# Two projections of an attention block as three rounded passes, and GpSimd's images and the gate's steps in another order

## The reference, cut to what matters

```python
xn = layernorm(x) * ln1_scale + ln1_bias              # over the 64 channels
q, k, v = split(windows8x8(xn) @ w_qkv + b_qkv)       # 8 heads of depth 8
attn = softmax((q * scale) @ k.T + rel_bias)
x = x + (attn @ v) @ w_proj + b_proj
x = x + gelu(layernorm(x) @ w_mlp1 + b_mlp1) @ w_mlp2 + b_mlp2
h = pw1_w @ x + pw1_b
scores = sigmoid(relu(mean(h) @ fc1) @ fc2)           # the gate
mask = the 32 largest scores of 64 channels
h = relu(h); offsets = tanh(mean(h) @ off_w + off_b)
for size in (3, 5, 7):                                # 32 channels each
    w = base * (1 + sigmoid(offset)) + tanh(offset)
    outs.append(depthwise_conv(h * mask, w))
out = pw_w @ concat(outs) + pw_b + x
```

## Time and profile before

| what | us |
|---|---|
| median of three timed runs (lowest, highest) | 318.81 (318.21, 319.14) |
| the profiled execution | 315.38 |
| its span, first to last instruction | 313.6 |
| TensorE busy, share of the span | 268.7, 86% |
| VectorE busy | 226.6, 72% |
| ScalarE busy | 204.8, 65% |
| GpSimd busy | 157.1, 50% |
| convolution matmuls L1263, 528 of them | 75.5 |
| keys and queries, L945 and L950, 32 halves | 19.5 |
| mean granted TensorE clock | 0.965 of full speed |

### The profile page before, as it was taken

One profiled execution on the slowest core, in us unless ns is written; L12 is line 12 of the kernel. 1 busy time (PEld: TensorE's weight loads), 2 busy tenths in 40 slices (PEclk: granted clock), 3 DMA queues, 4 the chain that ended last, 5 costly groups with the idle time before them and its releaser, 6 DMA issues.

```text
span 313.6 us, 6648 instructions
## 1 busy us (share of the span) xinstructions
PE 268.7 (86%) x2486; PEld 213.1 (68%) x2486; DVE 226.6 (72%) x448; ACT 204.8 (65%) x331; POOL 157.1 (50%) x195
## 2 busy tenths in 40 slices
PE   0566868899999999999989899998699989599992
PEld 0344655777767677676867545654499989599992
DVE  2758629378787887878888554888998599978222
ACT  6667753667678596685845879986632752978800
POOL 5052545568678676875661708076860440444400
PEclk9985999999999999999999999999969999799998
DMA  6981258334434343453540000740417857398841
GB/s 160 192 171 45 74 124 176 81 86 103 95 84 88 80 100 73 89 111 82 104 93 15 2 0 2 161 96 0 117 19 141 195 119 161 93 175 170 176 79 33
DMA packets 35118, 31.06 MB, mean 99 GB/s; under 512 B 20816, under 2 KB 30032, under 8 KB 35088
## 3 DMA queue, kind: packets, MB, share of 16 engines
q1 hardware_dynamic: 30608, 23.55, 32.7%
q0 software_dynamic: 3392, 6.17, 11.4%
q10 hardware_dynamic: 1088, 0.94, 1.5%
HBM read 4.54 MB, written 2.10 MB: 21 GB/s over the span
## 4 chain that ended last, share of the span: by engine, by line
PE 38%; POOL 19%; DVE 14%; issue 11%; ACT 6%; SPq 5%; DMA 5%; DVEq 0%; POOLq 0%; ACTq 0%
PE psum L1263 18%; POOL parts L337 8%; POOL k_blocks L554 5%; PE psum L1002 4%; PE psum L1165 4%; POOL q_blocks L562 4%; SPq L449 3%; PE psum L1066 3%; DMA probs<-in_rel_flipped 3%; DMA k_heads<-k_parts 2%; DVE maxima L1413 2%; PE psum L923 2%; SPq L461 2%; POOL q_heads L389 1%; PE psum L976 1%
## 5 line engine op out<-in xcount | busy, mean ns | idle before, releaser
L1263 PE MATMUL psum<-shifted,conv_w 128*128 128x286 f32 x528 | 75.5, 305 | 4.8 <-ACT conv_w L852 4.7
L1263 PEld LDWEIGHTS psum<-shifted,conv_w 128*128 128x128 f32 x528 | 73.7, 198 | 5.5 <-issue 4.0
L1002 PE MATMUL psum<-q_heads,k_blocks 128*128 128x256 f32 x384 | 62.1, 300 | 4.0 <-ACT probs L710 2.2
L1002 PEld LDWEIGHTS psum<-q_heads,k_blocks 128*128 128x128 f32 x384 | 51.3, 189 | 14.9 <-ACT probs L710 6.3
L710 ACT ACTIVATE probs<-psum 128x512 f32<-128x512 f32 x64 | 37.6, 606 | 10.1 <-PE psum L1002 9.1
L1413 DVE TENSOR_REDUCE maxima<-psum 128x8 f32<-128x512 f32 x64 | 40.3, 679 | 4.9 <-PE psum L976 4.9
L337 POOL TENSOR_TENSOR conv_w<-whole_w,conv_w 128x1408 fp32r<-128x1408 f32 x6 | 19.3, 3220 | 43.8 <-ACT conv_w L846 43.8
L554 POOL DMA_DIRECT2D k_blocks<-k_parts x56 | 32.2, 582 | 7.0 <-PE psum L1002 7.0
L337 POOL TENSOR_TENSOR parts<-square_logvar,parts 128x512 fp32r<-128x512 f32 x13 | 19.0, 1459 | 28.8 <-ACT square_logvar L723 15.8
L337 POOL TENSOR_TENSOR parts<-x,parts 128x256 fp32r<-128x256 f32 (+1 forms) x21 | 19.6, 944 | 26.6 <-ACT parts L659 19.5
L923 PE MATMUL psum<-parts,center_average 128*128 128x512 f32 x64 | 23.9, 458 | 10.2 <-DVE parts L337 8.2
(11 more groups left out here) (154 smaller groups left out, 499.4 us busy)
## 6 DMA issues: line engine op xcount, KB each, us to landing
shifted<-images SPq DMA_DIRECT2D x32, 243.8 KB, 4.5
q_heads<-q_parts SPq DMA_DIRECT2D x128, 32.0 KB, 2.5
k_blocks<-k_parts POOLq DMA_DIRECT2D x56, 64.0 KB
k_heads<-k_parts SPq DMA_DIRECT2D x64, 32.0 KB, 2.3
out<-x SPq DMA_DIRECT2D x8, 256.0 KB, 3.3
q_blocks<-q_parts POOLq DMA_DIRECT2D x28, 64.0 KB, 2.5
conv_w<-conv_w SPq DMA_DIRECT2D x10, 176.0 KB, 3.4
x<-in_x SPq DMA_DIRECT2D x6, 256.0 KB, 5.0
```

The costliest lines, as they stand in the source:

```text
L1002: ins = pe.matmul(bank[:, hh * G // 2:(hh + 1) * G // 2], k_blocks[:, hh, w // (NW // 2), k_part, w % (NW // 2), :], q_heads[:, w // (NW / ...
L1263: ins = pe.matmul(psum[:, CONV[bh][g], 0:SPAN], conv_w[bh][:, w_part, h * NSLOT + slot, :], shifted[:, bh, part, stream, first:first + SPA ...
```

## The change

**Three passes.** A new tensor qk_parts holds the rounded and the remaining part of the query and key weights; VectorE makes it once, before step 0. For groups 2 to 7 keys and queries are three f32r passes: high weights by high data, high by low, low by high. For this ScalarE copies normed to normed_high between its seventh and eighth exponential of a step, and VectorE subtracts to get normed_low between its seventh and eighth maximum. The keys wait for dv_normed_low. Groups 0 and 1 and all values are as before. The space comes from the first 288 columns of the constants, which now go to scratch memory that the probabilities take later.

**Four ReLU buffers.** relu(n) writes to one of four halves (square_logvar and square_logvar2), and waits for images three behind.

**GpSimd.** Images 0 to 3, no_row(1), then a wait for the whole weights of unit 1 (dv_whole 2), images 4 and 5, the low part of unit 2, images 6 and 7, the low part of unit 3.

**Gate steps.** On TensorE, ScalarE and VectorE some steps of gates 1 and 2 stand elsewhere, and add_mlp(7) and low_weights(0, 1) too.

The diff, cut to its core:

```diff
         mlp1_w = sb("mlp1_w", [128, 2, HIDDEN], F32R)
+        qk_parts = sb("qk_parts", [128, 2, 2, 128], F32R)
         qkv_bias = sb("qkv_bias", [128, 3])
...
         projected = square2
+        normed_high, normed_low = (at(n, [128, G], F32R) for n in ("normed_high", "normed_low"))
         inv_sum = at("inv_sum", [128, 2 * 4 * T // 32, 2])
...
 
+        def relu_half(n):
+            return (square_logvar, square_logvar2)[n // 2 % 2][:, n % 2, :]
+
         def pointwise_bank(n):
...
             def low_image(n, b4, half):
-                odd, even = (relu_out[:, half, q * G // 2:(q + 1) * G // 2] for q in range(2))
+                odd, even = (relu_half(n)[:, q * G // 2:(q + 1) * G // 2] for q in range(2))
                 pool.wait_ge(S["ac_relu"], n + 1)
...
                 pool.tensor_tensor(pair_columns(0, b4, half), by_rows(odd), by_rows(even), ALU.add).then_inc(S["po_pairs"], 1)
-                pool.tensor_tensor(columns(1, b4, half), by_rows(relu_out[:, half, :]), columns(0, b4, half).bitcast(F32), ALU.subtract)
+                pool.tensor_tensor(columns(1, b4, half), by_rows(relu_half(n)), columns(0, b4, half).bitcast(F32), ALU.subtract)
                 pool.wait_ge(S["po_pairs"], n + 1)
...
             no_row(0)
-            for n in range(5):
+            for n in range(4):
                 low_image(n, n // 2, n % 2)
...
             no_row(1)
-            for n in range(5, NG):
+            pool.wait_ge(S["dv_whole"], 2)
+            for n in range(4, 6):
                 low_image(n, n // 2, n % 2)
...
             for u in range(2, B):
+                if u == 3:
+                    for n in range(6, NG):
+                        low_image(n, n // 2, n % 2)
                 bh = u % 2
...
                 act.activation(rstd[:], logvar, ACT.Exp, scale=-0.5).then_inc(S["ac_rstd"], 1)
+
+            def high_of_normed(n):
+                act.wait_ge(S["dv_normed"], n + 1)
+                act.wait_ge(S["pe_q"], n)
+                act.copy(normed_high[:], normed[:]).then_inc(S["ac_normed"], 1)
 
...
                 exponentials(g, 6)
+                if far is not None:
+                    high_of_normed(far)
                 exponentials(g, 7)
...
                 act.wait_ge(S["pe_pw1"], n + 1)
-                act.wait_ge(S["po_images"], n + NBORDER - 1)
+                act.wait_ge(S["po_images"], NBORDER if n < 4 else n + NBORDER - 3)
                 if n == 2 * NIMAGE:
...
                 bank = psum[:, pointwise_bank(n), :]
-                act.activation(relu_out[:, half, :], bank, ACT.Relu, bias=vec[:, 9:10], accum_out=r_sum[:, n:n + 1])
+                act.activation(relu_half(n), bank, ACT.Relu, bias=vec[:, 9:10], accum_out=r_sum[:, n:n + 1])
                 act.activation(columns(0, b4, half), by_rows(bank), ACT.Relu, bias=vec[:, 9:10]).then_inc(S["ac_relu"], 1)
...
             odd_high(0, 0, range(1))
+            relu(6, 3, 0)
             gate(1)
-            relu(6, 3, 0)
             relu(7, 3, 1)
...
 
+            def multiply_normed(n, bank, which):
+
+                if isinstance(n, int) and n < 2:
+                    return pe.matmul(psum[:, bank, :], qkv_w[:, which, :], normed[:], start=True, stop=True)
+                pe.wait_ge(S["dv_qk_low"], 1)
+                pe.wait_ge(S["dv_normed_low"], n - 1)
+                for w_part, part in ((0, 0), (0, 1), (1, 0)):
+                    ins = pe.matmul(psum[:, bank, :], qk_parts[:, w_part, which, :], (normed_high, normed_low)[part][:], start=w_part + part == 0, stop=w_part == 1)
+                return ins
+
             def keys(n):
...
                     pe.wait_ge(S["dv_max"], NW * (n - 1) + 6)
-                pe.matmul(psum[:, MISC1, :], qkv_w[:, 1, :], normed[:], start=True, stop=True).then_inc(S["pe_k"], 1)
+                multiply_normed(n, MISC1, 1).then_inc(S["pe_k"], 1)
 
...
                     pe.wait_ge(S["ac_log2"], n - 2)
-                pe.matmul(psum[:, MISC0, :], qkv_w[:, 0, :], normed[:], start=True, stop=True).then_inc(S["pe_q"], 1)
+                multiply_normed(n, MISC0, 0).then_inc(S["pe_q"], 1)
 
...
             mlp2(6, 0)
+            mlp2(7, 1)
             gate_means(1)
-            mlp2(7, 1)
+            pointwise1(6, 0)
             gate_scores(1)
-            pointwise1(6, 0)
 
...
             pointwise1(7, 1)
-            gate_spread(1)
             passes(0, 0, 1)
             passes(0, 0, 2)
+            gate_spread(1)
             gate_sums(2)
...
             passes(1, 0, 2)
+            gate_scores(2)
             low_passes(0, 1)
-            gate_scores(2)
-            high_passes(1, 0)
+            high_weights_in(1, 0)
+            passes(0, 0, 0)
             gate_spread(2)
+            passes(0, 0, 1)
+            passes(0, 0, 2)
             low_passes(1, 0)
...
 
+            def low_of_normed(n):
+                dve.wait_ge(S["ac_normed"], n - 1)
+                low_part(dve, normed[:], normed_high[:], normed_low[:]).then_inc(S["dv_normed_low"], 1)
+
             def k_low(n, par):
...
                             round_maxima(nxt, 0)
+                        if w == 6 and far is not None:
+                            low_of_normed(far)
                     round_maxima(nxt, 1)
...
             k_low(1, 1)
+            dve.tensor_copy(qk_parts[:, 0], qkv_w[:, 0:2, :]).then_inc(S["dv_qk_high"], 1)
+            dve.wait_ge(S["dv_qk_high"], 1)
+            low_part(dve, qkv_w[:, 0:2, :], qk_parts[:, 0], qk_parts[:, 1]).then_inc(S["dv_qk_low"], 1)
             step(0, 1, 2, None, None, 0)
...
             low_weights(0, 0)
+            add_mlp(7)
             gate_hidden(1)
-            add_mlp(7)
+            products(0, 1)
             gate_scores(1)
-            products(0, 1)
+            add_products(0, 1)
             gate_spread(1)
-            add_products(0, 1)
+            low_weights(0, 1)
             gate_mask(1)
             gate_taps(1)
-            low_weights(0, 1)
             gate_means(2)
...
             add_products(1, 1)
+            gate_mask(2)
             result(0, 1)
-            gate_mask(2)
             gate_taps(2)
...
                 for bh in range(2):
```

23 lines of the change are left out of this document (12 added, 11 removed).

## The result

The changed kernel takes 321.87 us in the median of 20 runs (317.94 to 328.08), against 318.64 for the kernel before in the same comparison (20 runs, 313.23 to 320.60). The ratio is 1.016, with a 95% interval of 1.0121 to 1.0199, so it is slower by 3.9 to 6.3 us. The ratio is that of the fast runs alone, those within 1.5% of the fastest of their kernel, and so it is not the quotient of the two medians, which lie 3.2 us apart. The profiled executions agree with it: 320.44 us with a span of 318.6, against 315.38 with a span of 313.6. The sum on record said +3.0.

A forecast was written before the change was run, and what follows sets the result against it. Taken as bounds: in the loop VectorE's queue of maxima, then TensorE, then ScalarE; before the end VectorE's queue. Sum: 318.81 + 2.8 (loop) + 0.2 (tail) = 321.8 us, chance 0.47; 8-in-10 range 316.0 to 325.2.

The forecast's parts named there:

- The direction and the path: Whole kernel: slower, chance 0.65; loop step set by VectorE's queue of maxima, then TensorE, then ScalarE.
- The loop term, +2.8: Attention loop: the subtraction ahead of the keys delays each step by 0.55 us, over five borders.
- The bound of 6.5: Loop term's upper bound: 5 x 1.3 us, from the rival where GpSimd's subtraction gets between VectorE's two halves.
- The first border: Loop, step 0 to 1: the delay is absorbed because TensorE waits 1.76 us there for the queries' DMAs.
- "Worse" by GpSimd between the halves: Loop steps 2 to 5: GpSimd's shifted subtraction splits VectorE's two, 1.3 us a step, 324.2 us; chance 0.14.
- TensorE sets the loop: Loop rival: each of ten shorter products gives 0.15 us, 1.5 in all, time 317.5 us; chance 0.10.
- The tail term, +0.2,: After the loop: moved images, gate order and early scores sum to +0.2 us, bounds -7.0 and +3.4.
- moved images: Tail: GpSimd's images 4 to 7 at new places, -1.4 and -4.0 us saved, +3.2 and +4.0 us paid.
- mask ahead of the result: Tail: gate_mask(2) ahead of result(0, 1) on VectorE meets GpSimd's low part of unit 3, +1.0 us.
- early scores: Tail: gate_scores(2) earlier on TensorE removes VectorE's 3.11 us wait, a new wait costs about 0.5: -2.6 us.
- the order around the second gate and the early spread: Tail: new order of gate steps, given no term of its own, priced only through the images its instructions meet.
- The single signs: Trace signs: steps 19.2 us, add_products(0, 0) 2.6, gate_spread(2) with add_products(1, 1) over 7, last 264 matmuls about 3 later.

The follow-up runs named there:

- a1: Changed kernel with the old tail (two ReLU buffers, images in one row, old gate order), three passes kept: 321.66 us, ratio 1.0177 to the kernel before.
- a3: Changed kernel with keys and queries as full products that still wait for the now unused subtraction: 322.18 us against 316.00 for the kernel before.
- b1: Changed kernel with the subtraction three maxima earlier and ScalarE's copy one exponential earlier: 316.79 us, ratio 0.9989 to the kernel before.
- b2: Changed kernel with full keys, three passes for queries only, subtraction behind the eighth maximum: 313.32 us, ratio 0.9865 to the kernel before.
- a4: Changed kernel with six unused passes of 512 columns added ahead of the keys: 318.62 us, ratio 1.0088 to the kernel before.
- c4: Changed kernel with three unused passes of 512 columns added ahead of the keys: run once, span 316.5 us against 318.6 for the changed kernel.
- b4: Changed kernel with the old loop (full products) and GpSimd's images back in one row: run once, span 309.6 us against 313.6 before.
- a2: Changed kernel with the old loop (full products, no rounded copy or subtraction), new tail kept: 316.46 us against 316.00 for the kernel before.

## Why the prediction was right, and where it was not

**The direction and the path** held. What bounds the loop is the seam of VectorE's maxima, TensorE and ScalarE, and an instruction put ahead of the keys lengthens it; a1 and a3 show that, b1 takes most of it away by moving the subtraction (with ScalarE's copy), and b2 all of it, with keys that don't need the subtraction.

**The loop term, +2.8, was mis-sized; it measured +7.2.** Two steps of it failed.
- The delay. From the first maximum to the keys I had 1.16 more, and a1's undisturbed step has 1.19. What is given back behind the keys I put at 0.6, from "keys of 0.7 to the next instruction" and 0.15 for the queries; the three passes took 0.85 to the next instruction, and from keys to the next step's first maximum the trace gives back 0.35 (70.36 to 84.29, against 70.02 to 84.30). So 0.8 a step and not 0.55: over five borders 4.0, less the 0.4 by which step 1 began its maxima earlier than before (65.29 and 65.70).
- The clock. The price of the keys' wait was taken as its length alone. In four of the steps that count the clock fell behind it, at 0.9 each, 3.6 in all. Together 7.2. a4 and c4, which change nothing but TensorE's rest, remove exactly this second part.
The bound of 6.5, which I drew from another mechanism, was passed by 0.7.

**The first border** held for the rows on record: the first step grew by only 0.29 (50.75 to 70.02 became 51.23 to 70.79), and the wait of 1.76 for the queries' DMAs is gone.

**"Worse" by GpSimd between the halves** did not happen in the changed kernel: there is no wait for GpSimd ahead of the variance of steps 2 to 5, where the kernel before waits 0.43. "TensorE sets the loop" could not act while the keys waited for VectorE. With nothing in the way (b2) the queries' shorter product gives 0.19 a step, near the 0.15 that this rival counted with; the place of the subtraction kept it out.

**The tail term, +0.2,** came out at -0.77 against the profile of before, and at +0.2 against the tail of a1, which is the same code. That the sum fits a1 is luck, since its parts don't: moved images +1.8 forecast, +2.06 measured (b4 against a2); mask ahead of the result +1.0, measured 1.20 with late images and 0.81 with early ones; early scores -2.6, measured -1.4; the order around the second gate and the early spread nothing, which is -2.2 (or -1.25 against a1) as the remainder, so that the parts add up by construction. The last two are misses of opposite sign. The step that failed for the scores was to take the whole wait of 3.11 in the earlier trace rows as theirs: with the scores late and the new order, 1.99 of it stands. For the second gate, I had priced its instructions only through the images they meet.

**The single signs**: `add_products(0, 0)` takes 2.60 (220.40 to 223.00), as said. `gate_spread(2)` with `add_products(1, 1)` takes 6.77 (252.15 to 258.92), of which 0.49 is a wait for ScalarE, where I said over 7. The mask's blocked operation takes 2.62, where I said one would wait, at 2.8. The last 264 matmuls start 6.39 later than 271.46, where I said about 3, and steps are 20.35 long instead of 19.2, both by the loop term.
The row at 261.61 shows more than the operations with both inputs in SBUF on which I had counted. By the Trainium skill (SBUF — State Buffer, Who interferes with whom) copies and scalar operations can contend with GpSimd's too, when their operands meet the conditions of a mode that uses two ports. The trace agrees: a TENSOR_SCALAR with one small input took 2.62 and ended with GpSimd's operation.

**The last stretch** was no term of my sum. It gave 1.39 back, because the clock fell at the fourth unit and not at the fifth; the changed tail has it both ways (a2, b1), so this is not the work of the change.

**That 321.8 was near the median of 321.87** is thus largely luck. The sum was +3.0 and the interval of the ratio says +3.9 to +6.3. In the profiled pair the loop's +7.2 is met by -0.8 and by -1.4 that I had not foreseen, and the span is 318.6 where I had 316.6.

## What to carry to other kernels

Where an operation is split so that its parts are cheaper, find the place of the helper operation before counting what the parts save: here three cheaper passes for each of two products saved 0.24 us a step, and the subtraction that feeds them, standing right ahead of TensorE's next instruction, cost 1.0. Three maxima earlier it costs 0.35, and in a wait that VectorE has anyway nothing. A wait on TensorE is to be priced at its length and, as a second case, with the work behind it at half the clock.
Moving GpSimd's work out of VectorE's way needs a new place in which VectorE doesn't work in SBUF; here the new places cost 2.06 more than the old (b4 against a2).
Compare stretches between marks, not spans, where the clock or DMAs make spans differ by more than the edit, and look at the clock inside the stretch too.
